# Cross attention of a decoder block: three output tiles in the ring, O in the fourth step, key weights of one half, and another order on ScalarE and VectorE

## The reference

```python
def _L0_xattn_ref(text_hidden, vision_tokens, vision_mask, Wq, Wk, Wv, Wo):
    ...
    q = (text_hidden @ Wq).reshape(B, T_text, N_HEADS, HEAD_DIM).transpose(0, 2, 1, 3)
    k = (vision_tokens @ Wk).reshape(B, T_vis, N_KV_HEADS, HEAD_DIM).transpose(0, 2, 1, 3)
    v = (vision_tokens @ Wv).reshape(B, T_vis, N_KV_HEADS, HEAD_DIM).transpose(0, 2, 1, 3)
    k = jnp.repeat(k, GROUPS, axis=1)
    v = jnp.repeat(v, GROUPS, axis=1)
    scores = jnp.einsum('bhtd,bhsd->bhts', q, k) / scale
    ...
    attn = jax.nn.softmax(scores, axis=-1)
    ...
    out = jnp.einsum('bhts,bhsd->bhtd', attn, v)
    out = out.transpose(0, 2, 1, 3).reshape(B, T_text, N_HEADS * HEAD_DIM)
    return out @ Wo
x = x + _L0_attn_ref(_layernorm(x, axis=-1), ...)
x = x + _L0_xattn_ref(_layernorm(x, axis=-1), ctx_1024, mask_BxS2_bf1, ...)
x = x + _L0_ffn_ref(_layernorm(x, axis=-1), ...)
```

## Time and profile before

| what | value |
|---|---|
| runs | 2688.05 us median of 3 (2687.05 to 2689.24) |
| the profiled execution | 2685.35 us, span 2683.7 us |
| PE, PEld busy | 2482.7 us (93%), 2257.6 us (84%) |
| VectorE, ScalarE, GpSimd busy | 1733.0 (65%), 1241.2 (46%), 1030.1 us (38%) |
| cross attention: first scores, scores of step 254, of step 255, closing O | 510.58, 2367.61, 2375.58, 2388.06 us |
| b = 30: step g2 starts; SP issues the ctxT load | 1408.11; 1408.30 us |
| two-piece copies of o | 352 copies where 256 would be whole |
| GpSimd waits for VectorE's maximum | 864.9 us |

### The profile page before, as it was taken

The page is one execution under the profiler, slowest core; times in us unless marked ns, Lnnn a source line. Parts: engine busy times, 40 slices in busy tenths (PEclk is TensorE's granted clock), DMA queues, the critical chain, the costliest instruction groups (busy, mean ns, idle before and its releaser), DMA issues. The chain is left out here.

```text
span 2683.7 us, 46237 instructions
## 1 busy us (share of the span) xinstructions
PE 2482.7 (93%) x14850; PEld 2257.6 (84%) x14851; DVE 1733.0 (65%) x4899; ACT 1241.2 (46%) x3183; POOL 1030.1 (38%) x1424
## 2 busy tenths in 40 slices
PE   6899897799999999999999999999999999979488
PEld 5888886788989898889989898898989888869376
DVE  7878886565575657566575756656565665644466
ACT  4555553454454545445454545445454454522211
POOL 4334443243343434334353534334343343431422
PEclk9999998899999999999999999999999999975699
DMA  8322332412122112212121211111111111122654
GB/s 256 95 71 84 96 108 89 162 50 66 62 75 66 62 54 74 74 52 83 52 91 58 88 55 53 54 41 55 51 57 54 53 55 41 41 72 70 220 178 129
DMA packets 108892, 217.87 MB, mean 81 GB/s; under 512 B 20336, under 2 KB 48720, under 8 KB 108416
## 3 DMA queue, kind: packets, MB, share of 16 engines
q1 hardware_dynamic: 103440, 188.42, 21.9%
q0 software_dynamic: 5040, 16.58, 1.7%
q10 hardware_dynamic: 224, 10.49, 1.2%
HBM read 134.57 MB, written 91.36 MB: 84 GB/s over the span
## 5 line engine op out<-in xcount | busy, mean ns | idle before, releaser
L1171 POOL TENSOR_SCALAR x_probs<-x_probs,x_inv 112x376 f32<-112x376 f32 x512 | 639.3, 1258 | 273.6 <-DVE x_inv L1323 273.6
L1165 POOL TENSOR_SCALAR x_bias<-x_top 112x1 f32<-112x1 f32 x512 | 129.1, 252 | 871.8 <-DVE x_top L1295 864.9
L1215 ACT ACTIVATE x_probs<-x_probs,x_bias 112x376 f32<-112x376 f32 x512 | 307.0, 603 | 105.2 <-POOL x_bias L1165 104.7
L1380 PE MATMUL x_ps_o<-x_pT,x_v 128*128 128x224 f32 (+1 forms) x2304 | 310.3, 279 | 43.2 <-DVE x_pT L1302 42.5
L1380 PEld LDWEIGHTS x_ps_o<-x_pT,x_v 128*128 128x128 f32 (+1 forms) x2304 | 288.0, 192 | 69.6 <-DVE x_pT L1302 61.5
L1380 PE MATMUL x_ps_f<-x_xT,x_wq 128*128 128x448 f32 x1536 | 339.3, 371 | 4.5 <-issue 4.5
L1380 PE MATMUL x_ps_f<-x_wo,x_oT 128*128 128x512 f32 x1344 | 315.7, 391 | 1.0 <-DVE x_oT L1311 1.0
L1380 PE MATMUL x_ps_s<-x_kT,x_qT 128*112 128x376 f32 x1536 | 314.6, 340 | 1.5 <-DVE x_top L1295 1.5
L1380 PE MATMUL x_ps_f<-x_ctxT,x_wk 128*128 128x376 f32 x1536 | 306.4, 335 | 1.9 <-DVE x_ctxT L1272 1.9
L1380 PEld LDWEIGHTS x_ps_f<-x_xT,x_wq 128*128 128x128 f32 x1536 | 282.4, 189 | 26.5 <-issue 4.7
L1380 PEld LDWEIGHTS x_ps_f<-x_wo,x_oT 128*128 128x128 f32 x1344 | 252.6, 189 | 50.0 <-issue 1.2
(11 more groups left out here) (186 smaller groups left out, 3799.5 us busy)
## 6 DMA issues: line engine op xcount, KB each, us to landing
x_ctxs<-x_ctxT SPq DMA_DIRECT2D x32, 752.0 KB, 3.8
x_ctxT<-x_ctxs SPq DMA_DIRECT2D x32, 752.0 KB, 4.3
x_xT<-h2T SPq DMA_DIRECT2D x16, 896.0 KB, 5.0
m_rows<-slots SPq DMA_DIRECT2D x35, 258.0 KB, 3.0
slots<-w_blank SPq DMA_DIRECT2D x8, 1032.0 KB, 5.2
x_ctxn<-in_ctx_dram SPq DMA_DIRECT2D x32, 256.0 KB
m_hn<-in_L_ffn_W_dram SPq DMA_DIRECT2D x32, 256.0 KB
w_xa<-in_x_dram SPq DMA_DIRECT2D x32, 224.0 KB, 3.3
```

Of the source, the lines that this page charges most:

```text
L1165: pool.tensor_scalar(bias[:, m:m + 1], top[:, m:m + 1], -0.1 * NEG, -SCALE, ALU.max, ALU.mult) \
L1171: pool.tensor_scalar(probs[0:T, m, 0:SE], probs[0:T, m, 0:SE], inv[:, m:m + 1], None, ALU.mult).then_inc(normed, 1)
L1215: act.activation(probs[0:T, m, 0:SE], probs[0:T, m, 0:SE], ACT.Exp, bias=bias[:, m:m + 1], scale=SCALE, accum_out=total[:, m:m + 1]).then_ ...
L1380: last = pe.matmul(out, w, r, start=m == 0, stop=m == len(jobs) - 1)
```

## The change

It does five things. (1) RING is three tiles. (2) C goes from g3 to g2 and O from g2 to g3. (3) wk holds one half; its pieces are by head (n) and not by channel block; the second half's are loaded at b = 30, each once the last K of the first half has used the old one, and split one step later each. (4) On ScalarE exps come first in a step, on VectorE maxima and then inverses; fills follow, out comes ahead of the sum of O, and x pieces and weight splits stand last. The mask row of the next batch is made at the end of g1. (5) The x pieces are in g1 and g2 of the batches with b % 4 of 1 and 2, and not in the four steps of b % 4 = 1.

```diff
-    RING = 2 * P
+    RING = 3 * P
...
-        if g == 3 and b + 2 < B:
+        if g == 2 and b + 2 < B:
             out += [("C", b + 2, 0), ("C", b + 2, 1)]
-        if g == 2 and b in TILE_OF:
+        if g == 3 and b in TILE_OF:
...
-    PIECES = {"k": CC, "v": CC, "q": KC, "o": H // 2}
+    PIECES = {"k": G, "v": CC, "q": KC, "o": H // 2}
...
-        if b == B - 8 and g < CC:
-            return [("k", 1, g)]
+        if 0 <= i - G * (B - 2) - 1 < G:
+            return [("k", 1, i - G * (B - 2) - 1)]
...
-        return b // QUAD + 1 if b % QUAD == 1 and b // QUAD + 1 < NB // QUAD else None
+        if b // QUAD + 1 == NB // QUAD or b % QUAD not in (1, 2) or g not in (1, 2):
+            return None
+        return b // QUAD + 1, 2 * (b % QUAD - 1) + g - 1
...
-        wk = sb("wk", [P, HALVES, 2, CC, G * D], F32R)
+        wk = sb("wk", [P, 2, CC, G * D], F32R)
...
# SP
-                    if b == B - 12:
-                        for n in range(PIECES["k"]):
-                            load_w(("k", 1, n))
...
+                    if b == B - 2:
+                        for n in range(PIECES["k"]):
+                            sp.wait_ge(fill_ready, until(("K", B - 1, n)))
+                            load_w(("k", 1, n))
...
# ScalarE
                 for i in range(STEPS):
-                    for p in splits_at(i):
-                        split(p)
+                    exps(i)
                     for f in early_fills(i):
                         if f[0] != "O":
                             fill(f)
-                    exps(i)
-                    if x_piece(i) is not None:
-                        split_x(x_piece(i), i % G)
                     if i >= 2:
                         out(i - 2)
...
                     for f in behind_transposes(i):
                         fill(f)
+                    if x_piece(i) is not None:
+                        split_x(*x_piece(i))
+                    for p in splits_at(i):
+                        split(p)
...
# VectorE
+                mask_row(0)
                 for i in range(STEPS):
-                    if i % G == 0:
-                        mask_row(i // G)
                     maxima(i)
-                    for p in splits_at(i):
-                        split(p)
+                    inverses(i)
                     for f in early_fills(i):
                         if f[0] != "O":
                             fill(f)
-                    inverses(i)
-                    if x_piece(i) is not None:
-                        split_x(x_piece(i), i % G)
+                    if i >= 2:
+                        out(i - 2)
                     for f in early_fills(i):
                         if f[0] == "O":
                             add(f)
-                    if i >= 2:
-                        out(i - 2)
...
                     for f in behind_transposes(i):
                         fill(f)
+                    if i % G == 1 and i // G + 1 < NB:
+                        mask_row(i // G + 1)
+                    if x_piece(i) is not None:
+                        split_x(*x_piece(i))
+                    for p in splits_at(i):
+                        split(p)
...
# PE
-                        slot = at % 2 * P
+                        slot = at * P % RING
```

More of the change, by code:

```diff
@@ L884, in cross_attention @@
     TILES = B * T // P
-    RING = 2 * P
+    RING = 3 * P
     SCALE = float(1.0 / np.sqrt(D))
     mdt = mask.dtype
-    assert B * T % RING == 0 and B % QUAD == 0 and SE > S and T * 2 <= RING
+    assert B * T % P == 0 and B % QUAD == 0 and SE > S and T * 3 <= RING
     def last_batch(tile):
@@ L940, in pieces_of @@
         return [(0, n, at)] + ([(n, T, 0)] if n < T else [])
-    PIECES = {"k": CC, "v": CC, "q": KC, "o": H // 2}
-    FIRST_SPLITS = [("k", 0, n) for n in range(CC)], [("q", 0, n) for n in range(KC)], [("v", 0, n) for n in range(CC)]
+    PIECES = {"k": G, "v": CC, "q": KC, "o": H // 2}
+    FIRST_SPLITS = [("k", 0, n) for n in range(G)], [("q", 0, n) for n in range(KC)], [("v", 0, n) for n in range(CC)]
     def splits_at(i):
@@ L1028, in weight @@
             kind, half, n = piece
-            return [{"k": lambda: wk[:, half, a, n, :], "v": lambda: wv[:, a, n, :], "q": lambda: wq[:, a, n, :],
+            return [{"k": lambda: wk[:, a, :, n * D:(n + 1) * D], "v": lambda: wv[:, a, n, :], "q": lambda: wq[:, a, n, :],
                      "o": lambda: wo[:, a, 2 * n:2 * n + 2, :]}[kind]() for a in (HI, LO)]
@@ L1033, in weight_source @@
             kind, half, n = piece
-            if kind in "kv":
-                return (Wk if kind == "k" else Wv)[n * P:(n + 1) * P, half * G * D:(half + 1) * G * D]
+            if kind == "k":
+                return Wk[:, (half * G + n) * D:(half * G + n + 1) * D].rearrange("(c p) d -> p c d", p=P)
+            if kind == "v":
+                return Wv[n * P:(n + 1) * P, half * G * D:(half + 1) * G * D]
             if kind == "q":
@@ L1370, in _, with weights @@
                 seen = [0]
-                def weights(kind, half):
-                    n = split_all(kind, half)
+                def weights(kind, half, piece=None):
+                    n = split_all(kind, half) if piece is None else SPLIT_NO[kind, half, piece] + 1
                     if seen[0] < n:
@@ L1395, in fill @@
                         half = at // B
+                        weights("k", half, n)
                         if n == 0:
-                            weights("k", half)
                             if half:
@@ L1401, in fill @@
                                 pe.wait_ge(fill_done, until(("C", at, 1)))
-                        last = product(out[:, 0:SE], [(wk[:, half, a, c, n * D:(n + 1) * D], ctxT[:, at % 2, b_, c, :])
+                        last = product(out[:, 0:SE], [(wk[:, a, c, n * D:(n + 1) * D], ctxT[:, at % 2, b_, c, :])
                                                       for c in range(CC) for a, b_ in PASSES])
```

## The result

| | before | after |
|---|---|---|
| runs, beside each other on one chip | 2687.55 us median of 6 (2684.76 to 2689.24) | 2696.69 us median of 6 (2692.87 to 2700.00) |
| ratio after / before | | 1.0034, 95% interval 1.0023 to 1.0045 |
| the same pair on another occasion (e9, below) | 2686.44 us, 21 runs | 2699.89 us, 5 runs; 1.0048, 1.0035 to 1.0061 |
| profiled execution, its span | 2685.35, 2683.7 us | 2695.29, 2693.6 us |
| first scores, scores of step 254, of step 255, closing O | 510.58, 2367.61, 2375.58, 2388.06 us | 510.12, 2378.50, 2381.70, 2396.99 us |

The changed kernel is slower by 9.1 us, 0.34%, where +8 was forecast, in the range and in the likeliest case.

The account below looks back on a forecast made before the run. PE was taken to bound the cross attention. Steps +10 (excess 62.4 to 72.5), drain −2.5 and head +0.7 sum to +8, 2696 us; range 2681 to 2707, likeliest case 2694 to 2701 (0.40).

Parts of the forecast that it names:

- Order on ScalarE and VectorE: Cross attention steps: K copy behind exps and inverses lengthens the chain from maximum to product from 3.77 to 4.36 us.
- The 0.5 in 23 batches: g1 behind an O step: the sum into x_sums ahead of pT delays the product 0.5 us, 11.5 us in all.
- Batches without O: Every eighth batch, g2, g3 and g0 all short: products wait in three steps, 18.8 us over six such batches.
- The three fill banks: Fills wait for the third fill before: first Q of g2 1.34 us, 7 times (9.4); K of g3 4.2 us.
- faster: Rival: bank waits do not show and the key piece is early, giving 2679 us; chance 0.19.
- Weight splits: Pieces split at ends of short steps, batches 0 to 2, 32 to 34 and b = 29: 20.4 us, bounds 14 to 26.
- no change: Rival: splits and batches without O at their low ends (14 and 15), 2686 to 2693 us; chance 0.29.
- Key weights in one half: At b = 30 g2, PE waits behind the key load: 3.25 us once, between 1 and 5.
- much slower: Rival: chain 0.2 longer, so g0's product waits too, and the b = 30 pause lowers the clock: 2704 us; chance 0.12.
- At the head: Ahead of the first scores: four key loads issued instead of two, taken as 0.7 us, from 0 to 1.6.
- The drain: Loop's end: O covers step 255, closing O 17.5 to 18.5 behind step 254 instead of 20.45; −2.5 us.
- Hidden, at nothing: Fewer copies of o, x pieces and mask moved: no cost; mask keeps 0.34, if wrong some 3 us more.

Follow-up runs that it names:

- e9: The changed kernel itself, nothing altered, measured once more on another chip: 2699.89 us, ratio 1.0048 to the kernel before.
- e1: Changed kernel with K and C copies back ahead of exps on ScalarE and between maxima and inverses on VectorE: 2644.85 us, ratio 0.9896.
- e2: Changed kernel with the sum of O into x_sums put ahead of the out copy on VectorE: 2669.94 us, ratio 0.9990.
- e7: Changed kernel with K and C copies ahead of exps and inverses only in g2 of batches with Q: 2672.16 us, ratio 1.0010.
- e11: Same kernel as e7, run again beside the changed kernel on one chip: 2687.84 us, ratio 1.0009.
- e4: Changed kernel with K and C copies ahead of exps and inverses, sum ahead of out, key splits one step later: 2633.17 us, ratio 0.9853.
- e8: e4 with the wo pieces split only at the end of g0, ahead of the step with V: 2628.58 us, ratio 0.9840.
- e3: Changed kernel with the second half's key weights split one step later each: 2680.58 us, ratio 1.0030.
- e10: Same kernel as e3, run again beside the changed kernel on one chip: 2694.31 us, ratio 1.0026.
- e6: Changed kernel with a ring of two, C in g3 and O in g2 as before, new order kept: 2711.46 us, ratio 1.0152.

## Why the prediction was right, and where it was off

**The sum.** +9.1 measured, +8 forecast: +12.0 in the 255 steps where 10 was said, −1.96 in the drain where −2.5 was said. These two do not add up to the 9.4 between the first scores and the closing O, for the prediction's sum counts one step twice: step 254 is the last of the 255, and the drain begins with it. That step lasts 7.97 before and 3.19 after; less its bare duration its share is +0.7, and without it the steps give +11.35. The rest of the profiled execution's difference (−0.5 at the head, +1.0 behind the closing O) is within what executions of one kernel differ by. So that the total came within 1.1 us is in part luck: the steps were 2.0 more than said and the drain gave 0.5 less, and the double count and the 0.7 taken for the head made up for 1.4 of it.

**The waits.** pT 30.1 (about 30 said), none in g0 of ordinary batches (0.0 to 0.13 of excess there), the first Q of g2 behind x_kT seven times. "Wrong if g2 of the Q batches keeps 9.18" did not come: it is 10.65. A batch without O loses 3.1 us in its three steps.

**Order on ScalarE and VectorE.** The chain of 4.36 measured 4.33. In e1 the early K and C copies give back all the bank waits and 33 of the 52 waits for pT, 41 us of excess with all that hangs on it. This is the step on which the forecast stood, and it held.

**The 0.5 in 23 batches.** Held: 0.44 to 0.58, and e2 takes it away by moving the sum alone. 11.5 was said for 23; 20 batches have 9.7, and b = 62, in the table's last row, has 0.57. The other two stand in the rows of splits: at b = 33 g1 moving the sum alone gave back 0.9 (e2), at b = 30 g1 0.1.

**Batches without O.** 18.4 for 18.8, step by step as forecast.

**The three fill banks.** Mis-sized by a little: 1.45 in place of 1.34. The K copy was done when I said and Q starts 1.34 late, but the first Q behind the wait then runs 0.14 longer (2.74 for 2.60), which I had left out. e7 and e11 measured the term by itself: 10.4 us of excess, 12 us of time with wide intervals. The rival "faster", which rested on these waits not showing, falls here.

**Weight splits.** 22.2 for 20.4, inside 14 to 26. The rival "no change" needed 14 here and 15 for the batches without O.

**Batches 62 and 63.** 0.4 for −1, a term whose working the prediction does not show: b = 62 g1 has its 0.57, and the three steps of b = 63 that count here, which have no K, are −0.4 together.

**Key weights in one half.** The pause was 3.2, forecast 3.25. Four loads landed in 2.1 to 4.2 us; the first was issued at 1419.35, behind the loads of ctxT and mask, and its split began 4.24 later. The fit of the Trainium skill, DMA: Bandwidth & Descriptors, "Anatomy of one DMA", gives 2.3 us for 128 KB, and with it a pause of 1.8, as an estimate. The trace has more; but the page gives the fit for GpSimd's loads, and this one is SP's and had 752 KB under way beside it, so the trace does not test the fit. What failed in this term is the price of the pause: it was taken as idle time alone. The granted clock was 0.50 for the 3 us after it, 1.5 us more, and the term measures 4.7 where 3.25 was said. The trace of the kernel before already showed such a price: at b = 29 g1 PE paused 1.93 for pT, and the product behind it took 2.25 where 1.16 to 1.27 is usual, at a granted clock of 0.53 from 1374 to 1376. From the timeline of PE of that kernel:

```profile
1374.06 2.25 PE L1380 MATMUL x_ps_o<-x_pT,x_v 128*128 128x224 f32 x9 [1.93 <-DVE x_pT L1302]
```

The fall of the clock was in the rival "much slower" ("lowers the clock as the drain did"), where I had tied it to a second mechanism, a chain 0.2 longer, that did not come.

**At the head.** 0.7 was taken for four key loads in place of two. It can't be read: the first scores stand at 510.12 and 511.78 in the two profiles of the changed kernel, and at 510.45 to 514.71 in its versions, whose head is the same. The scatter is larger than the term, which stays open.

**The drain.** 18.49, the upper end of what was said. Behind the covering O, the product of step 254 waits 1.72 for its pT, and 0.5 of that is the sum of that O, which stands ahead of pT on VectorE: where e2 moves the sum the same wait is 1.21, and the closing O comes 14.77 behind step 255 instead of 15.29.

**Hidden, at nothing.** The mask rows on VectorE:

```profile
L1288 DVE TENSOR_SCALAR x_mrow<-x_mraw 112x375 f32<-112x375 uint8 x64 | 22.1, 346 | 0.0
```

All 64 last 344 to 351 ns, and none lies beside a normalising instruction of GpSimd; before they took 343 to 507, 400 in the mean: 345 to 347 the 16 that met none, 419 in the mean the 48 that did. So the new place spares some 3.5 us of VectorE, and its cover held. By the Trainium skill, GPSIMD Engine Reference, "Specifications", the two engines share their SBUF interfaces, with contention for VectorE instructions in a 2-port perf mode or with two SBUF inputs. The trace agrees in that the rows slow down beside GpSimd and not elsewhere; in which mode they ran it does not show.

## What to carry to other kernels

Where two engines copy what a third waits for, ask of each copy what is queued ahead of it: a copy put behind a chain of other engines' work (exps, then inverses) inherits that chain's end, and with three banks in turn the third fill behind pays for it. The same copy put where the engine waits anyway leaves none of these bank waits; moved in one step of sixteen it gave 0.4% here, in all of them 1.4%. And place and order are to be judged together, and an order part by part: the new places gained 0.8% under the old order, the whole new order lost 1.5% in the old places, and the best kernels (e4, e8) have the new places, the K and C copies and the sum where they were, and mask rows, x pieces and splits late in the step. A pause costs more than its idle time where the granted clock falls behind it.

## What the runs showed of the hardware

Pauses of PE of 2.9 to 3.0 us in a stretch at full clock were each followed by a granted clock of 0.50. In the changed kernel, e1, e7, e9 and e11 that lasted for some 3 us and put 1.4 to 1.7 us on g3 of b = 30 (0.06 in e3, e4 and e10, where the pause was gone). In e2 the same pause of 2.97 was followed by 0.50 from 1422 to 1428, and g3 lost 2.7. Shorter pauses went both ways: 1.93 in the kernel before (b = 29) and 1.75 in e9 (b = 33, a clock of 0.51 from 1520 to 1522) were followed by a fall, 1.81 in the kernel before (b = 33) and 1.77 in the changed kernel (b = 0) were not. So the length of the pause alone does not tell.

The head scatters with its clock. Where the mean granted clock up to 500 us is 0.94 (the changed kernel, e3, e4, e9) the first scores stand at 510.12 to 511.78, where it is 0.92 (e7, e10, e11) at 513.26 to 514.71, and where it is 0.93 (e1, e2, e6, e8) at 512.68 to 513.16, with the same program up to there. So 3 us between two profiled executions can come from the head alone.

In the drain the clock falls at different moments, in executions of one kernel too. Behind the scores of step 255, in stretches of 4 us, e9 and e11 keep 1.00 through 16 us, the changed kernel's first profile and e7 through 12 (0.99 and 0.96 in the fourth stretch, then 0.59 and 0.61), while e3 and e10 have 0.78 and 0.88 in the third and 0.50 in the fourth. That moves the closing O by 1.5 to 2.2 us. Why e3 and e10 were the early ones was not found; both split the keys late, but so do e4 and e8, which keep 1.00 through 12 and 16 us.

The chips differ clearly in one part: from the closing O to the end of the span it is 278.9 to 284.5 us on the two chips where the kernel before takes 2671 to 2673 us, and 294.6 to 297.5 where it takes 2686 to 2688. The cross attention's steps agree within what their excess tells. The cause in that last part was not looked for, and it falls on both kernels of each comparison.
